# Extra identity products on TensorE between and inside the attention stages of a two-layer vision kernel

## The chip, the cores and the metric

The kernel runs on 1 core of one Trainium2 chip. The metric is device time in microseconds (us) for one execution over a batch of 8 images, the median of several runs. The engines are TensorE (PE; its weight loads are PEld in the profile), VectorE (DVE), ScalarE (ACT), GpSimd (POOL) and SyncE (SP), which issues the DMAs.

## The reference, cut to what matters

Layer 0 is a linear attention with a 5x5 depthwise convolution. Layer 1 is a sparse-linear attention, and all that is changed lies in it:

```python
qkv = einsum('oc,bcl->bol', qkv_w, xf)          # 4 heads of 64, 4096 tokens, 64 blocks of 64
blk_scores = einsum('bhnd,bhmd->bhnm', qb, kb)  # block means
_, lut = top_k(blk_scores, 6)
s = einsum('bhnqd,bhnkd->bhnqk', qr, kg) * scale
o_s = einsum('bhnqk,bhnkd->bhnqd', softmax(s), vg)     # over the 6 chosen blocks
kvb = einsum('bhmkd,bhmke->bhmde', softmax(k), vr)
kv_q = einsum('bhnm,bhmde->bhnde', 1 - sel, kvb)       # over the 58 others
o_l = num / (den + EPS)                                # softmax(q) times kv_q
o = einsum('oc,bcl->bol', out_w, o_s + proj(o_l))
```

All is f32.

## The kernel before

The program is written per engine; each engine runs its own list, and semaphores with counts order them. The outer loop runs over pairs of images; inside it both images are unrolled, and in each image layer 0, then layer 1 with four heads one after the other: 32 heads in a run. One head of layer 1 has these stages on PE, in `tensor`:

1. Tokens: 16 steps over 256 tokens each: q, k, v by eight f32 instructions (L778) into banks 0 and 1 of PSUM, and two steps later `turn` (L755, L762), which transposes q, k and their softmax features and forms the products of keys and values of each block for the linear part.
2. Waits: for `s_raw` (ACT has copied the last tokens out of banks 0 and 1), `s_tbe`, `s_kvd`, and for the first head of an image `s_sel`, followed there by two transposes of the selection (L797), whose result the second scores wait for.
3. `scores(0)` and `scores(1)` (L818): each four products of 64x64 by 192 columns, each product from gathered keys and values. The gathers go into four buffers: POOL copies six pieces (L561), ACT two, DVE four (both through their copy helpers, L982 and L1144). For steps from 4 on they wait for `s_o` of the step four before.
4. `complements()` (L847): 65 products of 64x64 by 64 columns, weights read from KVM with a stride of 65, in alternating halves of the output partitions, after eight DMAs have brought `kv_rows` back to SBUF (`s_rel`). ACT and DVE copy the result out by banks 4 to 7.
5. 32 softmax steps, in software pipeline: `scores(p)`, `turn_probs(p-1)` (L838, from step 8 on with a `turn_out`, L825) and `apply(p-2)` (L878 twelve and L884 four instructions). DVE takes the maxima (L1379), ACT the exponentials (L1088), ACT copies the turned probabilities (L982), `apply` raises `s_o`, for which DVE's, ACT's and POOL's gathers wait. Every third step DVE normalises (L1391, L1393, L1395).

DVE's order in a step is: load offsets, maxima(p), gather(p+2), and every third step normalise. ACT's is: copy probabilities (p-1), load offsets, exp(p), copy an output, gather(p+2).

Of the kernel before, what the change touches and what calls it, by code (L numbers as in the profile page):

```python
# [32 lines left out]
CH = 512  # L33
# [6 lines left out]
NP = NBLK // 2  # L40
# [57 lines left out]
def build(nc, x, w0, taps, wp, w1, wo, lw, lb, consts, out, n_batch):  # L98
    with ExitStack() as ctx:
# [3 lines left out]
        def sem(name):  # L103
            return ctx.enter_context(nc.semaphore(name))
# [7 lines left out]
        ident, same8, same_head = CST[:, 0:P], CST[:, P:2 * P], CST[:, 2 * P:3 * P]  # L112
# [10 lines left out]
        PS = ctx.enter_context(nc.psum_tensor("PS", [P, 8, CH], F32))  # L123
# [80 lines left out]
        def chunk_of(tile, c):  # L204

            f = 2 * c
            oy, ox = f // 8, (f % 4) // 2
            return tile.rearrange("p (f r c) -> p f r c", f=PL, r=PW)[:, f:f + 2, oy:oy + R, ox:ox + R]
# [81 lines left out]
        s_pt = sem("probs_stored")  # L290
# [31 lines left out]
        def settle(eng):  # L322

            eng.sem_inc(s_settled, 1)
# [248 lines left out]
        def _(pe):  # L574
            pe.wait_ge(s_w, 16 * 7)

            for h in range(NH):
                last = nc.tensor.matmul(PS[:, h // 2, (h % 2) * C:(h % 2 + 1) * C], lhsT=arena[0:D, 0:P],
                                        rhs=WO[0:D, h, :], start=True, stop=True)
            last.then_inc(s_wo, 1)  # L580
            for ot in range(KT):
                for h in range(NH):
                    last = nc.tensor.matmul(PS[:, 2 + ot, 0:1], lhsT=WO[0:D, h, ot * P:(ot + 1) * P],
                                            rhs=LB[0:D, :], start=(h == 0), stop=(h == NH - 1))
# [11 lines left out]
            with pe.Fori(0, n_batch // 2) as pair:  # L596
                for half in range(2):
# [12 lines left out]
                    for g in range(2):  # L610
# [67 lines left out]
                        for j in range(3):  # L678
                            for c in range(NCH):
# [5 lines left out]
                                for kt in range(KT):  # L685
                                    last = nc.tensor.matmul(bank(i),  # L686
                                                            lhsT=W0[:, kt, (2 * j + g) * P:(2 * j + g + 1) * P],
                                                            rhs=XN[:, kt, c * CH:(c + 1) * CH],
                                                            start=(kt == 0), stop=(kt == KT - 1))
# [10 lines left out]
                        for c in range(NCH + 2):  # L700
                            if c < NCH:
                                attend(1, c)
                            if c >= 2:
                                i = base + att_item(1, c - 2) + 1
                                pe.wait_ge(s_free[1], b * IT + 2 + count(i, 1))
                                for ot in range(KT):
# [3 lines left out]
                                                     rhs=chunk_of(RAW[0], c - 2), start=True, stop=False)  # L710
                                    hand(i, nc.tensor.matmul(bank(i), lhsT=WP[:, 2 + g, ot * P:(ot + 1) * P],
                                                             rhs=AGG[0][:, (c - 2) * CH:(c - 1) * CH],
                                                             start=False, stop=True))
# [21 lines left out]
                    for hp in range(2):  # L735
                        wait_emptied(pe, b, L0_ITEMS + D_ITEMS * hp - 1)
                        settle(pe)
                        for h in (2 * hp, 2 * hp + 1):
                            hd, hl = b * NH + h, h % 2

                            def turn(p):

                                pe.wait_ge(s_nrm, hd * TP + p + 1)
                                if p == 0:
                                    pe.wait_ge(s_scc, b + 1)
                                if p >= 2:
                                    pe.wait_ge(s_tbe, hd * TP + p - 1)
                                if p % 2 == 0 and p >= 4:
                                    pe.wait_ge(s_kvd, hd * 8 + p // 2 - 1)
                                if p == 2 and hl == 1:  # L750
                                    pe.wait_ge(s_one, hd * NP)
                                sg = SG[p % 3]
                                for u in range(2):
                                    for s in range(2):
                                        nc.tensor.transpose(PS[:, 2 + p % 2, (2 * s + u) * P:(2 * s + u + 1) * P],  # L755
                                                            sg[:, (4 * u + 2 * s) * D:(4 * u + 2 * s + 2) * D], ident)
                                at = 6 - 2 * (p // 2 % 2)
                                for u in range(2):
                                    j = 2 * (p % 2) + u
                                    for odd in range(2):  # L760
                                        rows = slice(D * odd, D * (odd + 1))
                                        last = nc.tensor.matmul(PS[D:P, at + odd, j * D1:(j + 1) * D1],  # L762
                                                                lhsT=sg[rows, (4 * u + 3) * D:(4 * u + 4) * D],
                                                                rhs=twos[rows, 2 * p + u, 0, D:KVW],
                                                                start=True, stop=True)
                                last.then_inc(s_tb, 1)

                            for p in range(TP):
# [6 lines left out]
                                for u in range(2):  # L775
                                    t = 2 * p + u
                                    for kt in range(KT):
                                        last = nc.tensor.matmul(  # L778
                                            PS[:, p % 2, u * 3 * D:(u + 1) * 3 * D], lhsT=XN[:, kt, t * P:(t + 1) * P],
                                            rhs=W1[:, kt, h, :], start=(kt == 0), stop=(kt == KT - 1))  # L780
# [5 lines left out]
                            turn(TP - 2)  # L786
                            turn(TP - 1)

                            pe.wait_ge(s_raw, (hd + 1) * TP)
                            pe.wait_ge(s_tbe, (hd + 1) * TP)  # L790
                            pe.wait_ge(s_kvd, (hd + 1) * 8)
                            if h == 0:
# [49 lines left out]
                            def complement(r, at, bank):  # L842
                                for k in range(8):
                                    for side in range(2):
                                        e = 16 * r + 8 * side + k
                                        if e < D1:
                                            last = nc.tensor.matmul(  # L847
                                                PS[D * side:D * (side + 1), bank, (at + k) * NBLK:(at + k + 1) * NBLK],
                                                lhsT=KVM[:, :, e], rhs=COMP[:, h * NBLK:(h + 1) * NBLK],
                                                start=True, stop=True)  # L850
                                last.then_inc(s_cq, 1)

                            def complements():
                                for k in range(8):
                                    pe.wait_ge(s_rel[k], (hd + 1) * 16)
                                pe.wait_ge(s_cmp, b + 1)
                                settle(pe)
                                for r in range(4):
                                    complement(r, 0, 4 + r)
                                pe.wait_ge(s_kqa, hd * 4 + 3)  # L860
                                pe.wait_ge(s_kqd, hd * 5 + 3)
                                settle(pe)
                                complement(4, 0, 6)
                                pe.wait_ge(s_kqa, hd * 4 + 2)
                                pe.wait_ge(s_kqd, hd * 5 + 2)

                            def apply(p):
                                pe.wait_ge(s_pt, hd * NP + p + 1)
                                t = p // 3
                                if p == 0:  # L870
                                    pe.wait_ge(s_kqa, (hd + 1) * 4)
                                    pe.wait_ge(s_kqd, (hd + 1) * 5)
                                if p % 3 == 0 and t >= 2:
                                    pe.wait_ge(s_on, hd * TRIOS + t - 1)
                                at = p % 3 * 2 * D1
                                for i in range(3):
                                    for blk in range(2):
                                        nc.tensor.matmul(  # L878
                                            PS[D * blk:D * (blk + 1), 6 + t % 2, at:at + D1],
                                            lhsT=PT[p % 2][:, i * P + D * blk:i * P + D * (blk + 1)],  # L880
                                            rhs=G[p % GD][:, blk, i, D:KVW], start=(i == 0), stop=(i == 2))
                                for blk in range(2):
                                    n = 2 * p + blk
                                    last = nc.tensor.matmul(  # L884
                                        PS[D * blk:D * (blk + 1), 6 + t % 2, at + D1:at + 2 * D1],
                                        lhsT=QO[hl][D:P, n * D:(n + 1) * D], rhs=KVQ[:, n, :],
                                        start=True, stop=True)
                                last.then_inc(s_o, 1)

                            for p in range(NP + 2):  # L890
                                if p < NP:
                                    scores(p)
                                if p == 1:
                                    complements()
                                if 1 <= p <= NP:
                                    turn_probs(p - 1)
                                if p >= 2:
                                    apply(p - 2)
# [9 lines left out]
                        for ot in range(KT):  # L908
                            for c in range(NCH):
                                i = L0_ITEMS + D_ITEMS * hp + NCH * ot + c  # L910
                                claim(i)
                                for hh in range(2):
                                    last = nc.tensor.matmul(bank(i), lhsT=WO[:, 2 * hp + hh, ot * P:(ot + 1) * P],  # L913
                                                            rhs=QO[hh][:, c * CH:(c + 1) * CH],
                                                            start=(hh == 0), stop=(hh == 1))
# [590 lines left out]
```

## Time and profile before

| | us |
|---|---|
| median of 3 runs | 9082.88 |
| lowest, highest | 9064.64, 9105.43 |
| profiled execution, its own time | 9057.69 |
| profiled execution, span | 9055.9 |
| mean granted clock of PE | 0.919 |
| PE busy | 7636.7 |
| DVE, POOL, ACT busy | 5037.9, 3786.7, 3520.5 |

The span reaches from the first to the last instruction of one profiled execution. A granted clock of 1.00 is 2.4 GHz, 0.50 is 1.2 GHz. Busy times of PE are of pipelined instructions whose ends are modelled, so a busy PE need not be one at its peak.

### The profile page before, as it was taken

To read this page: it belongs to the slowest core of one execution; us is meant where nothing else is said; L and a number is where in the kernel's file an instruction comes from. 1 tells how busy PE (TensorE), PEld (TensorE's weight loads), DVE (VectorE), ACT (ScalarE), POOL (GpSimd) and SP (SyncE) were. 2 spreads that over 40 slices of the span, in tenths; PEclk is the share of its full clock that TensorE was granted. 3 is DMA by queue.
4 is the path that set the end of the run, shared out by engine and by line. 5 is a ranking of instruction groups with operands and counts; after the bars stand their busy time and mean duration, and the time that the engine had idled before them with its cause. 6 is when DMAs were issued, how large, how long until landed. Compare 5 with 4: busy or idle time off the path is not lost.

```text
span 9055.9 us, 206227 instructions
## 1 busy us (share of the span) xinstructions
PE 7636.7 (84%) x65004; PEld 5190.5 (57%) x65004; DVE 5037.9 (56%) x11563; ACT 3520.5 (39%) x9207; POOL 3786.7 (42%) x10084
## 2 busy tenths in 40 slices
PE   8978799787997879978899778997789977799788
PEld 5655556555565555655555555565555555566555
DVE  3475644756447564475644756447564475644655
ACT  1145621445214552145521455215552155511555
POOL 2345533445334553345533444334443344533444
PEclk9988999888999889988999888998889988999888
DMA  3201122011220112201122111221112211122111
GB/s 101 65 16 26 41 87 65 16 26 38 89 65 16 27 42 85 65 18 26 51 75 65 21 22 49 77 65 21 23 53 73 65 22 22 57 68 65 24 20 55
DMA packets 398743, 431.90 MB, mean 48 GB/s; under 512 B 159184, under 2 KB 355984, under 8 KB 393296
## 3 DMA queue, kind: packets, MB, share of 16 engines
q1 hardware_dynamic: 397648, 418.42, 16.3%
q8 instruction: 550, 9.01, 0.4%
q14 instruction: 545, 4.46, 0.2%
HBM read 102.76 MB, written 67.63 MB: 19 GB/s over the span
## 4 chain that ended last, share of the span: by engine, by line
PE 54%; DVE 23%; issue 7%; DMA 6%; ACT 5%; DVEq 3%; SPq 1%; POOL 0%; ACTq 0%; POOLq 0%
PE PS L623 12%; PE PS L686 7%; DVE arena L1144 5%; PE PS L913 5%; DVE arena L1234 4%; PE PS L778 3%; PE PS L666 3%; PE PS L878 3%; PE PS L838 3%; PE PS L847 3%; DVE SM L1379 3%; ACT arena L1088 3%; DVEq L1367 2%; DMA kv_rows<-arena 2%; PE PS L654 2%
## 5 line engine op out<-in xcount | busy, mean ns | idle before, releaser
L982 ACT ACTIVATE arena<-PS 128x128 f32<-128x128 f32 (+5 forms) x4160 | 1552.0, 399 | 1947.5 <-PE PS L623 596.5
L561 POOL COPY arena<-arena 64x129 f32 x6144 | 1527.9, 291 | 1372.0 <-PE PS L884 1094.0
L485 POOL TENSOR_TENSOR arena<-arena 128x512 f32<-128x512 f32 x768 | 806.2, 1072 | 1459.5 <-PE PS L623 1443.6
L623 PE MATMUL PS<-arena 128*128 128x256 f32 x6144 | 1359.1, 379 | 46.4 <-DMA arena<-arena 46.3
L1144 DVE COPY arena<-PS 64x260 f32<-64x260 f32 (+2 forms) x1272 | 634.3, 515 | 1352.5 <-PE PS L623 524.7
L623 PEld LDWEIGHTS PS<-arena 128*128 128x128 f32 x6144 | 1155.4, 189 | 270.6 <-issue 98.0
L1144 DVE COPY arena<-arena 64x129 f32 x4096 | 840.9, 267 | 398.3 <-PE PS L884 285.9
L1234 DVE RECIPROCAL arena<-arena 128x512 f32<-128x512 f32 x256 | 857.5, 3350 | 119.1 <-ACT arena L1030 117.5
L818 PE MATMUL PS<-arena 64*64 64x192 f32 x8192 | 699.0, 386 | 256.9 <-POOL arena L561 242.0
L491 POOL TENSOR_TENSOR BUF<-BUF,arena 128x512 f32<-128x512 f32 x256 | 358.2, 1399 | 1282.3 <-ACT arena L1018 1282.3
L1379 DVE TENSOR_REDUCE SM<-PS 128x1 f32<-128x384 f32 x1024 | 570.6, 558 | 539.7 <-issue 434.3
L1088 ACT ACTIVATE arena<-PS,SM 128x384 f32<-128x384 f32 x1024 | 595.1, 581 | 638.9 <-DVE SM L1379 598.6
L778 PE MATMUL PS<-W,BUF 128*128 128x192 f32 x4096 | 818.7, 348 | 27.2 <-ACT BUF L1010 20.5
L778 PEld LDWEIGHTS PS<-W,BUF 128*128 128x128 f32 x4096 | 687.2, 197 | 63.2 <-ACT BUF L1010 21.2
L686 PE MATMUL PS<-BUF,W 128*128 128x512 f32 x1536 | 678.8, 604 | 37.5 <-DVE BUF L1207 33.7
L825 PE MATMUL PS<-CST,arena 128*128 128x128 f32 x1024 | 312.1, 337 | 415.9 <-ACT arena L1088 379.7
L838 PE MATMUL PS<-CST,arena 128*128 128x128 f32 x3072 | 589.2, 307 | 52.0 <-ACT arena L1088 51.2
L878 PE MATMUL PS<-arena 128*64 128x65 f32 x12288 | 632.8, 243 | 0.0
L538 POOL TENSOR_TENSOR arena<-arena,SM 128x256 f32<-128x256 f32 x512 | 314.4, 614 | 748.1 <-DVE SM L1322 746.7
L878 PEld LDWEIGHTS PS<-arena 128*64 128x64 f32 x12288 | 483.9, 149 | 196.1 <-issue 193.9
L1147 DVE TENSOR_SCALAR arena<-PS 128x256 f32<-128x256 f32 (+1 forms) x336 | 160.1, 477 | 733.0 <-PE PS L623 432.7
L666 PE MATMUL PS<-arena 128*128 128x512 f32 x1024 | 498.4, 608 | 68.8 <-DVE arena L1241 56.0
(102 smaller groups left out, 10563.4 us busy)
## 6 DMA issues: line engine op xcount, KB each, us to landing
arena<-arena SPq DMA_DIRECT2D x1024, 128.0 KB, 2.3
arena<-arena SPq DMA_DIRECT2D x768, 144.5 KB
BUF<-in_x SPq DMA_DIRECT2D x18, 2048.0 KB, 12.0
kv_rows<-arena SPq DMA_DIRECT2D x256, 130.0 KB, 3.5
arena<-kv_rows SPq DMA_DIRECT2D x256, 130.0 KB
out<-BUF SPq DMA_DIRECT2D x64, 512.0 KB, 2.6
arena<-in_taps SPq DMA_DIRECT2D x96, 288.0 KB, 3.6
W<-in_w SPq DMA_DIRECT2D x2, 768.0 KB, 5.8
```

The lines of the kernel that those rows point to most:

```text
L485: last = pool.tensor_tensor(o, tap, mix, ALU.mult)
L561: last = pool.tensor_copy(G[p % GD][0:D, j // 3, j % 3, :], KVB[0:D, bass.ds(off, KVW)])
L623: last = nc.tensor.matmul(bank(i)[:, a * 256:(a + 1) * 256], lhsT=TW[n % 2][:, a * CH + k * P:a * CH + (k + 1) * P], rhs=src[:, k // 2:k / ...
L686: last = nc.tensor.matmul(bank(i), lhsT=W0[:, kt, (2 * j + g) * P:(2 * j + g + 1) * P], rhs=XN[:, kt, c * CH:(c + 1) * CH], start=(kt == 0 ...
L778: last = nc.tensor.matmul(PS[:, p % 2, u * 3 * D:(u + 1) * 3 * D], lhsT=XN[:, kt, t * P:(t + 1) * P], rhs=W1[:, kt, h, :], start=(kt == 0) ...
L838: last = nc.tensor.transpose(PS[:, 4 + p % 2, i * P:(i + 1) * P], PR[p % 2][:, i * P:(i + 1) * P], ident)
L878: nc.tensor.matmul(PS[D * blk:D * (blk + 1), 6 + t % 2, at:at + D1], lhsT=PT[p % 2][:, i * P + D * blk:i * P + D * (blk + 1)], rhs=G[p % G ...
L982: return nc.scalar.activation(o, i, ACT.Copy)
L1088: nc.scalar.activation(PR[p % 2].rearrange("p (i s c) -> p s i c", i=3, s=2), PS[:, 2 * (p % 2):2 * (p % 2) + 2, 0:3 * D].rearrange("p s ( ...
L1144: return nc.vector.tensor_copy(o, i)
L1234: order.after(nc.vector.reciprocal(DN[c % 2], DN[c % 2]))
L1379: nc.vector.tensor_reduce(NM[:, p % 2:p % 2 + 1], PS[:, 2 * (p % 2):2 * (p % 2) + 2, 0:3 * D], AX.XY, ALU.max, negate=True).then_inc(s_nm, 1)
```

## The change

A helper `keep_clock(bank, n)` issues n f32 products of the 128x128 identity with its own first 112 columns into columns 400 to 511 of a bank of PSUM; nothing reads those columns. It is called with 20 products into bank 0 after the wait for `s_raw` that follows the last `turn` of each head, with 8 products into bank 7 at the head of `complements()`, and with 2 products into bank 6 or 7 in each `apply`, in front of the wait for `s_pt`, which moves behind the other waits of `apply`.

```diff
+                            def keep_clock(bank, n):
+                                for _ in range(n):
+                                    nc.tensor.matmul(PS[:, bank, 400:CH], lhsT=ident, rhs=ident[:, 0:CH - 400],
+                                                     start=True, stop=True)
+
                             pe.wait_ge(s_raw, (hd + 1) * TP)
+                            keep_clock(0, 20)
                             pe.wait_ge(s_tbe, (hd + 1) * TP)
...
                             def complements():
+                                keep_clock(7, 8)
                                 for k in range(8):
                                     pe.wait_ge(s_rel[k], (hd + 1) * 16)
...
                             def apply(p):
-                                pe.wait_ge(s_pt, hd * NP + p + 1)
                                 t = p // 3
                                 if p == 0:
                                     pe.wait_ge(s_kqa, (hd + 1) * 4)
                                     pe.wait_ge(s_kqd, (hd + 1) * 5)
                                 if p % 3 == 0 and t >= 2:
                                     pe.wait_ge(s_on, hd * TRIOS + t - 1)
+                                keep_clock(6 + t % 2, 2)
+                                pe.wait_ge(s_pt, hd * NP + p + 1)
```

## Rows read from the trace of the kernel before

**Rows 1.** The page: busy times, and the chain that ended last by engine

```profile
PE 7636.7 (84%) x65004; PEld 5190.5 (57%) x65004; DVE 5037.9 (56%) x11563; ACT 3520.5 (39%) x9207; POOL 3786.7 (42%) x10084
...
PE 54%; DVE 23%; issue 7%; DMA 6%; ACT 5%; DVEq 3%; SPq 1%; POOL 0%; ACTq 0%; POOLq 0%
```

**Rows 2.** Timeline of PE, third head of the first image: start, duration, idle before

```profile
884.82 1.12 PE L755 MATMUL PS<-CST,arena 128*128 128x128 f32 x4 [0.53 <-POOL arena L538]
...
891.66 0.92 PE L818 MATMUL PS<-arena 64*64 64x192 f32 x8 [5.10 <-POOL arena L561]
893.68 0.92 PE L818 MATMUL PS<-arena 64*64 64x192 f32 x8 [1.10 <-POOL arena L561]
896.32 8.00 PE L847 MATMUL PS<-arena 64*64 64x64 f32 x130 [1.72 <-DMA arena<-kv_rows]
...
907.25 0.92 PE L878 MATMUL PS<-arena 128*64 128x65 f32 x12
```

**Rows 3.** Windows (stretch, length; PE, PEld, DVE, ACT, POOL; PEclk, DMA, GB/s)

```profile
532.70:536.10 3.40, 3.40 (x12) 3.21 (x12) 2.40 (x18) 0.94 (x4) 0.92 (x3) 0.50 0.00 0
536.10:539.50 3.40, 3.40 (x33) 2.94 (x32) 2.79 (x10) 2.23 (x8) 1.55 (x5) 1.00 0.02 3
...
886.60:896.30 9.70, 1.84 (x16) 0.68 (x17) 4.11 (x16) 2.84 (x9) 5.49 (x23) 0.50 0.37 64
...
896.30:904.30 8.00, 7.98 (x131) 7.88 (x131) 2.24 (x4) 2.04 (x4) 1.48 (x6) 0.50 0.02 4
...
2033.40:2043.80 10.40, 9.98 (x94) 6.04 (x93) 5.35 (x20) 6.78 (x17) 3.26 (x14) 0.50 0.07 15
...
7353.40:7363.00 9.60, 8.42 (x94) 5.08 (x93) 5.24 (x21) 6.40 (x16) 2.94 (x12) 0.69 0.07 16
...
sum 318.50, PE 290.12 PEld 175.25 DVE 171.13 ACT 205.77 POOL 101.85; mean PE 9.07 PEld 5.48 DVE 5.35 ACT 6.43 POOL 3.18
...
4290.50:4357.30 66.80, 51.98 (x781) 34.66 (x781) 44.36 (x158) 46.67 (x132) 38.74 (x156) 1.00 0.06 12
...
8804.80:8881.00 76.20, 63.51 (x781) 42.30 (x781) 47.39 (x159) 46.70 (x132) 38.08 (x155) 0.78 0.05 11
...
sum 2220.90, PE 1749.97 PEld 1166.24 DVE 1447.10 ACT 1491.80 POOL 1236.05; mean PE 54.69 PEld 36.45 DVE 45.22 ACT 46.62 POOL 38.63
```

**Rows 4.** Products by themselves: two timeline rows, a source row, a window

```profile
524.61 3.67 PE L723 MATMUL PS<-arena,W 128*128 128x64 f32 x16 [4.27 <-DVE arena L1274]
...
880.69 0.60 PE L755 MATMUL PS<-CST,arena 128*128 128x128 f32 x4
...
L755 PE MATMUL PS<-CST,arena x2048: 272/273/477, 531.0 to 8924.7; 128*128 128x128 f32 x187
...
210.00:220.00 10.00, 10.00 (x219) 7.38 (x220) 3.79 (x10) 3.87 (x12) 0.00 (x0) 0.91 0.01 2
```

**Rows 5.** Timeline of PE and DVE, softmax steps of the third head, fourth image

```profile
4312.91 0.57 PE L878 MATMUL PS<-arena 128*64 128x65 f32 x12
...
4313.57 0.56 PE L818 MATMUL PS<-arena 64*64 64x192 f32 x8
...
4317.80 0.33 PE L825 MATMUL PS<-CST,arena 128*128 128x128 f32 x1 [0.99 <-ACT arena L1088]
...
4318.38 0.57 PE L878 MATMUL PS<-arena 128*64 128x65 f32 x12
...
4318.90 0.39 PE L818 MATMUL PS<-arena 64*64 64x192 f32 x2
...
4319.38 0.96 DVE L1144 COPY arena<-arena 64x129 f32 x4 [0.56 <-PE PS L884]
...
4320.43 0.57 PE L878 MATMUL PS<-arena 128*64 128x65 f32 x12
...
4320.91 0.56 DVE L1379 TENSOR_REDUCE SM<-PS 128x1 f32<-128x384 f32 x1 [0.57 <-issue]
...
4321.50 0.73 DVE L1144 COPY arena<-arena 64x129 f32 x4
```

## The prediction

> **What bounds the kernel now.** I began with the page: TensorE (PE) is busy 84% of the span and holds 54% of the chain that ended last, with VectorE (DVE) at 23%; the mean granted clock of PE is 0.92 of full speed [rows 1]. So I asked where the clock is at 0.5 and whether PE is what is waited for there. The timeline of PE through one head's change from tokens to attention shows it: after the last turned pair PE idles 5.1 us until GpSimd's (POOL's) gather frees the first scores, runs 0.9 us, idles 1.1, runs 0.9, idles 1.7 us for the last DMA of `kv_rows`, and then issues the 130 complement instructions in 8.0 us, then the first steps [rows 2]. The windows, made for each of the 32 heads, give the clock of each part: between tokens and complements 19 of 32 heads are wholly at 0.50 and the rest at 0.56 to 0.71; the complements are at 0.50 in all 32; the first four softmax steps are at 0.50 to 0.70; the other 28 are between 0.78 and 1.00 [rows 3]; one or two of each 32 stand there. Idleness lets the clock fall, and the complements, though PE shows busy for all of their 8 us, do not lift it. It rises only in the dense steps after them.
>
> In those 28 steps (66.8 us where the clock stays up [rows 3]) PE is not simply the bound. The timeline of three of them has DVE waiting on the products (`apply`), PE waiting on ScalarE's (ACT's) exponentials, and ACT on DVE's maxima [rows 5]: a ring over all three, 7.2 us for three steps (3 x 66.8 / 28).
>
> **The price of a product.** An f32 product is two matmul instructions (four score products show as x8), each with its weight load, and identity weights are 128 wide. Nearest rows [rows 4]: at low clock 16 instructions with 128x128 weights and 64 columns take 3.67 us, at most 0.23 us each, and 0.22 without the tail of the last; at full clock four transposes with 128 weights and 128 columns take 0.60, so (0.60 - 0.273) / 3 = 0.109 each. 112 columns lie between 64 and 128, so the load sets the pace in both. One product is 0.22 us at full clock and 0.43 at half: 20 products 4.4 or 8.7 us, 8 products 1.7 or 3.5, two products 0.44 or 0.87. Nothing is removed; 20 + 8 + 64 products times 32 heads add 2944 products, 5888 instructions.
>
> **The 20 products.** They follow the last `turn` directly (its copy was long done) and lie in the 5.1 us idle of PE. At full clock they fit: no cost. At half clock all 20 would end 3.6 us late. But they are a dense run of full-array products, of the kind under which the stretch 532.70 to 536.10, with PE 3.40 of 3.40 busy at 0.50, ended its low clock: the next stretch is at 1.00 [rows 3]; the forecast is that the clock comes back in their middle, so the first scores are about 1.5 us late, which the second scores, waiting for their own gather until 2.0 us later, take up. In the first head of a batch the transposes of SEL also move behind them; the second scores, which need their result, wait for POOL anyway. Cost nothing.
>
> **The 8 products.** From the end of the second scores to the complements is 1.7 us in the head shown. At full clock they fill it exactly; at half they make the complements 1.8 us late. The DMAs are on SP's queue and depend on nothing that moved. I take 0.4 us per head (some heads low, some with a shorter gap): +13 us. Bounds 0 and 58.
>
> **Complements at full clock.** No row shows it. Bounds: half of 8.0, 3.9 us, if the array sets their pace at both clocks; 130 x 45.7 ns = 5.9 us by the window at 210 us, where PE issues 219 mostly small matmuls in 10 us [rows 4]; 8.0 us if something unclocked (their weights are read with a stride of 65) sets it. The `apply` group of twelve took 0.92 us low and 0.57 at full clock [rows 2, 5], a ratio of 0.62, which would be 5.0. I take 4.9: 3.1 us less. It will not hold in every head: the clock can still fall between the first and second scores, or under the complements themselves, which have a quarter of the array each. For 0.88 of it: 2.7 us x 32 = -87 us. Bounds 0 and -125.
> The Trainium skill, "TensorE: Matmul & The Clock Gate", section "Wait — 56ns, not 53.3ns?", says that with hardware decode off the sequencer's microcode spends about 62 ns on each MATMUL and that this binds once the array work is shorter. By that rule the complements would take 130 x 62 ns = 8.1 us at either clock and the saving would be nothing; the 8.00 us measured at half clock agrees with it, the 45.7 ns of the window at 210 us does not.
>
> **The first four steps** took 318.5 us over 32 heads, 9.95 each; 10.4 where wholly low, 9.6 where low for 0.31 x 2 x 9.6 = 6.0 us [rows 3]. So a low us costs 0.8 / 4.4 = 0.18 us, and at full clock they would take 8.5; two of their three product pairs lie on the path, +0.9. I take a gain of 1.0: -32 us. Bounds 0 and -46.
>
> **The other 28 steps, clock.** Nine of the 32 stretches have a mean clock of 1.00 and take 66.5 to 67.9 us, mean 67.0; the longest, at 0.78, takes 76.2 [rows 3]. With PE busier the falls should go: 2220.9 - 32 x 67.0 = -77 us.
>
> **The other 28 steps, the two products.** Their cover would be PE's idle time, but they sit between `turn_probs` and `apply`, and `apply` waits for nothing there (18.38 after the turn at 17.80). In the ring I hold the turn at 4317.80 and walk on [rows 5]: `apply` 18.38 becomes 18.82 and ends 0.44 later, DVE's gather, idle 0.56 for it, goes from 19.38 to 19.82; the next maxima from 20.91 to 21.35, ending 21.91; the next `apply`, 20.43, becomes 20.87 to 21.0 and ends 21.70 to 21.9; the gather after it goes from 21.50 to 21.94. The third gather of the three comes late by DVE's own work (the normalisation), and has no wait that grows. So three steps cost at least 0.44; if the next scores start later after `apply` (0.66 as at 4312.91 to 4313.57, not 0.52 as at 4318.38 to 4318.90) PE makes the following turn late too, and it is 0.57. I take 0.50: 28 / 3 = 9.3 groups, 4.65 us a head, +149 us. Bounds: 0 if all is absorbed in PE's idle time (PE is busy 52.0 of 66.8 us), and 28 x 0.44 x 32 = +394 if every one is on the path; from the walk, 131 to 170.
>
> **Sum.** +13 - 87 - 32 - 77 + 149 = -34 us against the profiled execution, span 9055.9 of 9057.7 us. The median of the runs, 9082.9, is 25 us above it; the same difference gives 9049.
>
> **Rivals.** (1) The complements do not speed up. For: 8.00 us in every head and a strided weight load; against: the 45.7 ns window. The sum loses 87 us: 9136. (2) The clock falls again in the 3.6 us between the 20 products and the 8, in which PE runs only two score groups, and the half-speed 8 delay the complements. For: the low clock of the head shown is there in its last `turn` already (four transposes in 1.12 us), right after an idle time of 0.5 us [rows 2, 4]. Then no gain on complements, half of that on the first steps, and +1.8 x 32 = 58 instead of 13: 9049 + 87 + 16 + 45 = 9197. It ends slower, and decides once more than about half of the heads do it. (3) The pairs in the steps are absorbed, because PE, ACT and DVE regroup around them: a third of 149 is left, 9049 - 99 = 8950. For: PE's 14.8 us of idle per head in these steps; against: the walk. (4) Two or three crossings of the ring in three steps: 0.8 us per group, 0.3 x 9.3 x 32 = +89: 9138.
>
> **How the numbers follow.** Chances: forecast 0.50, its own range 9000 to 9095; rival 1 0.15; rival 2 0.12; rival 3 0.15; rival 4 0.08. The term that decides is a difference of 149 + 13 lost and 196 gained, so the middle is near no change. The range from rival 3 to just short of rival 2, 8955 to 9150, leaves out about 2 in 10. A measurement here tells 0.5%, 45 us. Faster (below 9037): rival 3 and 0.5 of the forecast's, 0.40. Slower (above 9128): rivals 1, 2 and 4 with a part of each inside, and the forecast's tail, 0.25. Within: 0.35.
>
> **What would show it.** In the changed profile: complements at clock 1.0 in most heads with a duration of 4 to 6 us; the first scores no later than before relative to the last turn; the 28 steps at clock 1.00 in nearly all heads, but 71 to 72 us long instead of 66.8; four or so new instructions ahead of each `apply`, 0.44 us between turn and `apply` added. Complements at 8.0 us with clock 1.0 say rival 1; at clock 0.5, rival 2; 28 steps at 68 us, rival 3; above 74, rival 4.

## The result and the profile after

The changed kernel takes 9222.3 us (median of 4 runs, 9202.0 to 9227.2) against 9076.4 us for the kernel before in the same comparison: ratio 1.0152, 95% interval 1.0122 to 1.0181. It is slower by 1.5%, where 9049 us and "near no change" were forecast, and it lies outside the range of 8955 to 9150. In the changed kernel the new products are L791, the scores L824, the turns L831 and L844, the complements L853 and `apply` L886 and L892; in the experiments the numbers move by a few lines.

The page of the changed kernel, busy times and chain:

```profile
PE 8114.3 (88%) x70892; PEld 5833.8 (63%) x70892; DVE 5070.5 (55%) x11563; ACT 3519.4 (38%) x9207; POOL 3801.9 (41%) x10084
...
PE 55%; DVE 23%; issue 8%; ACT 5%; DVEq 3%; DMA 3%; SPq 1%; POOL 1%; POOLq 0%; ACTq 0%
```

PE's mean granted clock rose from 0.919 to 0.952, PE is busy 478 us more, and the span is 160.8 us longer (9216.7). The higher clock did not shorten the run. The new products (L791) are 908.5 us of PE's busy time.

The timeline of PE in the third head again, start and duration, as in [rows 2]:

```profile
892.95 6.88 PE L791 MATMUL PS<-CST 128*128 128x112 f32 x40
899.75 1.03 PE L824 MATMUL PS<-arena 64*64 64x192 f32 x16
900.71 2.04 PE L791 MATMUL PS<-CST 128*128 128x112 f32 x16
902.95 7.94 PE L853 MATMUL PS<-arena 64*64 64x64 f32 x130 [0.19 <-issue]
910.82 0.55 PE L844 MATMUL PS<-CST,arena 128*128 128x128 f32 x3
911.29 0.56 PE L824 MATMUL PS<-arena 64*64 64x192 f32 x8
```

This is the picture that was hoped for: the 20 products (x40 instructions) begin at low clock and end at full, both score groups run in 1.03 us, the 8 products take 2.04, and the first turn takes 0.55. Only the complements are as long as ever: 7.94 us, where they took 8.00. The windows (columns as in [rows 3]) of this head's complements and first four steps, of another head's complements, and of the 28 steps of the head of [rows 5] are below; the sums are over the 32 heads, in this order: last turn to complements, first four steps, 28 steps:

```profile
902.90:910.90 8.00, 7.96 (x131) 7.92 (x132) 2.26 (x4) 2.06 (x4) 1.48 (x6) 1.00 0.02 5
...
910.80:919.70 8.90, 7.45 (x105) 5.38 (x104) 5.14 (x21) 6.79 (x17) 2.97 (x12) 1.00 0.08 18
...
2877.30:2885.40 8.10, 8.10 (x132) 7.98 (x132) 2.30 (x4) 2.09 (x4) 0.00 (x0) 0.71 0.01 2
...
4370.20:4442.40 72.20, 61.66 (x897) 47.39 (x897) 45.85 (x160) 46.70 (x132) 39.01 (x156) 1.00 0.05 12
...
sum 361.80, PE 309.92 PEld 278.89 DVE 144.46 ACT 90.83 POOL 214.23; mean PE 9.69 PEld 8.72 DVE 4.51 ACT 2.84 POOL 6.69
...
sum 339.60, PE 310.41 PEld 222.11 DVE 169.76 ACT 204.79 POOL 100.88; mean PE 9.70 PEld 6.94 DVE 5.31 ACT 6.40 POOL 3.15
...
sum 2328.00, PE 1970.07 PEld 1515.13 DVE 1473.43 ACT 1492.80 POOL 1247.01; mean PE 61.56 PEld 47.35 DVE 46.04 ACT 46.65 POOL 38.97
```

The same three sums before were 319.5 (the answer of the windows before, not shown ahead), 318.5 and 2220.9 [rows 3]. So the 161 us are: way to the complements +42, complements 0 (256.1 us over the 32 heads before, 256.6 after), first four steps +21, 28 steps +107, all the rest -10. Six of the 32 complement windows have clock 1.00, two 0.50, the others lie between; all take 7.9 to 8.1 us. Five heads have clock 1.00 through their first four steps as well, and take 8.5 to 8.9 us for them.

In the 28 steps the clock is at full speed nearly throughout, and the head of [rows 5] takes 72.2 us for 66.8. Two of its steps on the timeline, PE and DVE:

```profile
4399.36 0.33 PE L831 MATMUL PS<-CST,arena 128*128 128x128 f32 x1 [1.00 <-ACT arena L1096]
...
4399.85 0.60 PE L791 MATMUL PS<-CST 128*128 128x112 f32 x4
...
4400.38 0.57 PE L886 MATMUL PS<-arena 128*64 128x65 f32 x12
...
4401.38 0.94 DVE L1152 COPY arena<-arena 64x129 f32 x4 [1.00 <-PE PS L892]
...
4401.97 0.60 PE L791 MATMUL PS<-CST 128*128 128x112 f32 x4
...
4402.49 0.57 PE L886 MATMUL PS<-arena 128*64 128x65 f32 x12
...
4402.91 0.56 DVE L1387 TENSOR_REDUCE SM<-PS 128x1 f32<-128x384 f32 x1 [0.60 <-issue]
...
4403.50 0.74 DVE L1152 COPY arena<-arena 64x129 f32 x4
```

From the turn (4399.36) to `apply` (4400.38) it is now 1.02 us, where it was 0.58 (4317.80 to 4318.38 in [rows 5]): the pair's 0.44, as priced. DVE's idle time for `apply` grew from 0.56 to 1.00 us, the same 0.44. Nothing hides the pair: it lies on the ring of PE, DVE and ACT.

### The profile page after: what moved, and what is told of

It reads as the page before. It is cut to its first block, busy times and chain, and to the rows that moved or that the text cites. A ratio compares the mean times of both kernels' runs of the same rounds, so it can differ in the third digit from the quotient of the medians.

```text
span 9216.7 us, 217683 instructions
## 1 busy us (share of the span) xinstructions
PE 8114.3 (88%) x70892; PEld 5833.8 (63%) x70892; DVE 5070.5 (55%) x11563; ACT 3519.4 (38%) x9207; POOL 3801.9 (41%) x10084
## 4 chain that ended last, share of the span: by engine, by line
PE 55%; DVE 23%; issue 8%; ACT 5%; DVEq 3%; DMA 3%; SPq 1%; POOL 1%; POOLq 0%; ACTq 0%
PE PS L623 12%; PE PS L686 7%; DVE arena L1152 5%; PE PS L921 5%; PE PS L791 4%; DVE arena L1242 4%; PE PS L778 3%; DVE SM L1387 3%; PE PS L666 3%; PE PS L853 3%; PE PS L886 3%; ACT arena L1096 2%; PE PS L844 2%; DVEq L1375 2%; PE PS L654 2%
## 5 line engine op out<-in xcount | busy, mean ns | idle before, releaser
L1152 DVE COPY arena<-arena 64x129 f32 x4096 | 871.9, 274 | 447.3 <-PE PS L892 335.2
L791 PE MATMUL PS<-CST 128*128 128x112 f32 x5888 | 908.5, 293 | 0.0
L791 PEld LDWEIGHTS PS<-CST 128*128 128x128 f32 x5888 | 820.8, 209 | 16.9 <-issue 11.5
L824 PE MATMUL PS<-arena 64*64 64x192 f32 x8192 | 654.1, 352 | 49.3 <-POOL arena L561 25.0
L831 PE MATMUL PS<-CST,arena 128*128 128x128 f32 x1024 | 293.8, 318 | 351.9 <-ACT arena L1096 316.3
L844 PE MATMUL PS<-CST,arena 128*128 128x128 f32 x3072 | 541.7, 287 | 62.9 <-ACT arena L1096 62.1
L886 PE MATMUL PS<-arena 128*64 128x65 f32 x12288 | 595.7, 233 | 0.0
L990 ACT ACTIVATE arena<-arena 64x129 f32 x2048 | 519.3, 300 | 115.8 <-POOL arena L524 47.0
```

What stands on the lines that cost most here:

```text
L791: nc.tensor.matmul(PS[:, bank, 400:CH], lhsT=ident, rhs=ident[:, 0:CH - 400], start=True, stop=True)
L886: nc.tensor.matmul(PS[D * blk:D * (blk + 1), 6 + t % 2, at:at + D1], lhsT=PT[p % 2][:, i * P + D * blk:i * P + D * (blk + 1)], rhs=G[p % G ...
L990: return nc.scalar.activation(o, i, ACT.Copy)
L1152: return nc.vector.tensor_copy(o, i)
```

## The experiments

In all of them the ratio is to the kernel before, timed beside them.

**steps_only and front_only** split the change: the first takes out the 20 and the 8, the second the pair.

```diff
-                            keep_clock(0, 20)
-                                keep_clock(7, 8)
...
-                                keep_clock(6 + t % 2, 2)
```

> The change with the 20 and the 8 products taken out; only the pair ahead of each apply stays. Theory A (the pair lies on the ring of TensorE, VectorE and ScalarE): the 28 steps take 72 to 73 us per head at clock 1.00 as in the changed kernel, against 69.4 before, so +107 us, and the first four steps, still begun at low clock, cost up to 1 us more per head: ratio to the kernel before 1.012 to 1.016. Theory B (the loss lies in the 20 and 8 products, which make scores and complements late): the ratio is 1.00 to 1.005.

> The change with the pair in each apply taken out; the 20 and the 8 products stay. Theory A: the way from the last turn to the complements is 41 us longer over 32 heads as in the changed kernel, the complements stay at 8.0 us, the steps keep their low stretches: ratio 1.002 to 1.006. Theory B: the whole loss is here, ratio 1.012 to 1.016.

steps_only: 1.0116 (1.0092 to 1.0141). front_only: 1.0031 (1.0014 to 1.0049). Theory A holds: about four fifths of the loss is the pair in the steps. The 28 steps of steps_only, over 32 heads, and below them the same of front_only:

```profile
sum 2329.80, PE 1970.30 PEld 1515.85 DVE 1472.60 ACT 1491.44 POOL 1238.38; mean PE 61.57 PEld 47.37 DVE 46.02 ACT 46.61 POOL 38.70
```

```profile
sum 2227.40, PE 1758.88 PEld 1172.16 DVE 1443.89 ACT 1488.47 POOL 1237.43; mean PE 54.97 PEld 36.63 DVE 45.12 ACT 46.51 POOL 38.67
```

With the pair 72.8 us a head, without it 69.6. The first four steps, in the same order:

```profile
sum 349.90, PE 322.58 PEld 229.94 DVE 172.53 ACT 204.37 POOL 101.63; mean PE 10.08 PEld 7.19 DVE 5.39 ACT 6.39 POOL 3.18
```

```profile
sum 309.30, PE 276.58 PEld 167.29 DVE 169.50 ACT 207.22 POOL 100.03; mean PE 8.64 PEld 5.23 DVE 5.30 ACT 6.48 POOL 3.13
```

Against 318.5 before, the pair alone costs +31 us there, 0.98 us a head, and the 20 and the 8 alone, through the clock, bring only -9. Together that is the +21 of the changed kernel.

**step_one**: `keep_clock(6 + t % 2, 1)` in place of 2 in steps_only.

> steps_only with one product in place of two ahead of each apply. If the price is what lies between turn and apply on the ring, half of it: 28 steps of about 70 us (72.8 with two, 67.0 with none at full clock), ratio 1.003 to 1.007. If any product at this place costs (a wait, not a length), nearly 72.8 again and a ratio above 1.010.

1.0015 (1.0003 to 1.0027), less than expected; the 28 steps:

```profile
sum 2237.20, PE 1810.46 PEld 1333.31 DVE 1464.30 ACT 1490.92 POOL 1239.68; mean PE 56.58 PEld 41.67 DVE 45.76 ACT 46.59 POOL 38.74
```

That is 69.9 us a head. At full clock: 67.0 with none (the mean of the nine stretches of the prediction), 69.9 with one, 72.8 with two. The price is linear in the length, 2.9 us a head for 0.22 us, as if it were on the path in 13 of 28 steps (2.9 / 0.22), or 1.4 times in three.

**steps_moved** puts the pair where PE waits, without the 20 and the 8:

```diff
                             def turn_probs(p):
                                 x = p - TURN_LAG
-                                pe.wait_ge(s_p, hd * NP + p + 1)
                                 if p >= 2:
                                     pe.wait_ge(s_pt, hd * NP + p - 1)
                                 if x >= 2:
                                     pe.wait_ge(s_one, hd * NP + x - 1)
+                                keep_clock(4 + p % 2, 2)
+                                pe.wait_ge(s_p, hd * NP + p + 1)
...
-                                keep_clock(6 + t % 2, 2)
```

> No 20 and no 8 products; the pair of each step is moved from in front of apply to in front of turn_probs' wait for the exponentials (waits for the PSUM bank first), into the bank that the turn is about to overwrite. If what costs is the place between turn and apply, TensorE's idle time ahead of the turn (0.42 us per step in the kernel before) covers most of the pair, while the clock stays up: 28 steps of 67 to 69 us per head, ratio 0.990 to 0.999. If any pair in a step costs (TensorE is the bound by its load alone), 72 us again and a ratio of 1.012 or more.

0.9941 (0.9916 to 0.9965): the same number of products per step, 32 heads, and the sign turns. The 28 steps fall to 67.9 us a head, with no low clock left in them:

```profile
sum 2171.80, PE 2063.88 PEld 1523.30 DVE 1439.65 ACT 1478.28 POOL 1231.39; mean PE 64.50 PEld 47.60 DVE 44.99 ACT 46.20 POOL 38.48
```

PE is busier here than in steps_only (2064 against 1970 us) and the steps are 158 us shorter. So neither the load of PE nor the clock sets the loss, but the place of the pair between turn and `apply`.

**after_apply** issues the pair behind `apply`, also without the 20 and the 8:

```diff
-                                keep_clock(6 + t % 2, 2)
...
                                 last.then_inc(s_o, 1)
+                                keep_clock(2 * ((p + 1) % 2), 2)
```

> No 20 and no 8 products; the pair of each step is issued behind apply instead of ahead of it, into a free bank of the scores. Same instructions and the same load of TensorE as steps_only. If the ring turn, apply, gather is the price, it is gone here: 28 steps of 67 to 69 us, ratio 0.990 to 0.998. If the load of TensorE is, or the scores that now start 0.44 us later, 71 to 73 us and 1.008 to 1.013.

My expectation fell: 1.0326 (1.0308 to 1.0343), the slowest of all. The 28 steps take 75.0 us a head and the first four 13.8; the sums over 32 heads, 28 steps and then first four:

```profile
sum 2401.60, PE 2323.09 PEld 1663.08 DVE 1515.42 ACT 1476.20 POOL 1194.64; mean PE 72.60 PEld 51.97 DVE 47.36 ACT 46.13 POOL 37.33
```

```profile
sum 440.30, PE 426.95 PEld 278.60 DVE 184.25 ACT 218.55 POOL 133.59; mean PE 13.34 PEld 8.71 DVE 5.76 ACT 6.83 POOL 4.17
```

The timeline of PE, one step at full clock:

```profile
4454.28 0.57 PE L883 MATMUL PS<-arena 128*64 128x65 f32 x12
...
4454.77 0.33 PE L889 MATMUL PS<-arena 64*64 64x65 f32 x4
...
4455.04 0.70 PE L791 MATMUL PS<-CST 128*128 128x112 f32 x4
...
4455.67 0.56 PE L823 MATMUL PS<-arena 64*64 64x192 f32 x8
...
4456.15 0.33 PE L830 MATMUL PS<-CST,arena 128*128 128x128 f32 x1
```

From `apply` to the next scores it is 1.39 us (4454.28 to 4455.67), against 0.52 to 0.66 without the pair [rows 5]: a pair between two groups of 64x64 costs 0.73 to 0.87 us of PE, up to twice its 0.44 ahead of `apply`. The products start 0.27 us after the last 64x64 group started, where score groups overlap with it, and the scores wait 0.63 us from their start. In the stretch shown PE's own work repeats every 2.46 us (scores 4453.20 to 4455.67), 28 x 2.46 = 68.9 us, with no wait for another engine in it: here PE is nearly the bound. So this run does not test the ring; it tests the price of a product among small tiles, which I had taken from rows of full-array neighbours.

That price is not why this run is the slowest. The eleven heads whose 28 steps ran at clock 1.00 took 71.4 to 72.3 us, mean 71.7, a little less than the 72.8 of steps_only. The other 21 had mean clocks of 0.81 to 0.99 and took up to 83.6 us, and the first four steps, at 0.50 throughout in 21 heads, took 440.3 us against 349.9 of steps_only. In the first head a step at half clock took 4.07 us of PE (scores 595.36 to 599.43), where it took 2.46 at full. Why the clock stayed low for longer here is not shown.

**Fewer products, later.** moved_one is steps_moved with one product; moved_late has the pair and moved_one_late one product, both only from the fourth turn on (`if p >= 4:` ahead of `keep_clock`).

> As steps_moved (no 20, no 8, products in front of turn_probs' wait), with one product per step. If the clock is the only thing that helps, and one product is enough to hold it up, the 28 steps take at most the 67.9 us of steps_moved, at best 67.0, and the first steps lose less at low clock: ratio 0.990 to 0.994. If one is not enough, stretches with a clock below 1.0 come back and the ratio is between 0.994 and 1.0.

> As steps_moved, with the pair only from the fourth turn on. The turn behind the complements was 1.0 us later per head with the pair in front of it at low clock (8.92 from the first complement to the first turn, 7.93 before): that comes back, 32 us: ratio 0.990 to 0.992 (0.994 with it). If the early pairs pay for themselves by lifting the clock sooner, the ratio stays at 0.994 or above.

> One product per step, only from the fourth turn on. If both savings add: ratio 0.988 to 0.991, the fastest of all; 28 steps at 67.0 to 67.9 us.

moved_one: 0.9913 (0.9897 to 0.9930). moved_late: 0.9946 (0.9928 to 0.9964). moved_one_late: 0.9908 (0.9891 to 0.9925), 8968.7 us, the lowest median of the kernels that compute the reference, though not told apart from moved_one (8971.6). One product is enough: 28 steps at 67.1 us a head in both, sum for moved_one_late:

```profile
sum 2147.40, PE 1961.62 PEld 1362.71 DVE 1414.46 ACT 1491.00 POOL 1246.88; mean PE 61.30 PEld 42.58 DVE 44.20 ACT 46.59 POOL 38.97
```

Leaving out the early ones is worth nothing that can be told: the turn behind the complements comes 1 us sooner, but the first four steps are longer (331.9 against 320.7 us for the pair, 320.5 against 312.6 for one), because their clock comes back later. The expectation of 0.990 to 0.992 for moved_late was missed.

**sel_first** is front_only with `keep_clock(0, 20)` moved behind the waits for `s_tbe` and `s_kvd` and behind the transposes of the selection.

> front_only with the 20 products behind the transposes of the selection and behind the waits for s_tbe and s_kvd. If the longer way to the complements in the first head of each image (13.9 us against 10.1 before) comes from those transposes being queued behind the 20 products, that way shrinks to 10 to 11.5 us in these eight heads, and the ratio falls from 1.003 to 0.999 to 1.001. If it comes from the scores waiting for TensorE itself, it stays at 13 us or more and the ratio at 1.003.

1.0010 (0.9997 to 1.0022), with front_only at 1.0031. In the first head of the first image, changed kernel first, then sel_first:

```profile
569.51 4.72 PE L791 MATMUL PS<-CST 128*128 128x112 f32 x40
...
574.16 0.33 PE L803 MATMUL PS<-CST,arena 64*128 64x64 f32 x2
574.53 0.93 DVE L1368 TENSOR_SCALAR arena<-PS 64x64 f32<-64x64 f32 x4 [4.12 <-PE PS L803]
576.23 0.93 DVE L1152 COPY arena<-arena 64x129 f32 x4 [0.77 <-issue]
577.51 0.92 PE L824 MATMUL PS<-arena 64*64 64x192 f32 x8 [3.02 <-POOL arena L561]
...
579.82 3.75 PE L791 MATMUL PS<-CST 128*128 128x112 f32 x16
```

```profile
572.10 0.30 PE L802 MATMUL PS<-CST,arena 64*128 64x64 f32 x2 [1.12 <-DVE arena L1151]
572.33 4.72 PE L791 MATMUL PS<-CST 128*128 128x112 f32 x40
576.98 0.56 PE L824 MATMUL PS<-arena 64*64 64x192 f32 x8
578.66 0.56 PE L824 MATMUL PS<-arena 64*64 64x192 f32 x8 [1.12 <-POOL arena L561]
579.14 2.04 PE L791 MATMUL PS<-CST 128*128 128x112 f32 x16
581.11 3.16 PE L853 MATMUL PS<-arena 64*64 64x64 f32 x50
```

In the changed kernel the transposes (L803) stand behind the 20 products, DVE sits 4.12 us for them, and its four gathers for the first scores come behind the complement masks (L1368) on its queue. PE then idles 3.02 us ahead of the first scores, and the 8 products run at half speed, 3.75 us. With the order turned round the complements start 10.4 us after the last turn in these eight heads, on average, instead of 14.2 (10.2 before). In the other 24 heads, which have no such transposes, the way is 10.6 us against 10.2 in front_only, so part of the gain is lost there; the later start of the 20 products, behind the two other waits, was not tested by itself. (The trace puts the 3.02 us down to a gather of POOL; of the three gathers for the first scores DVE's ended last, at 577.16.)

**contig_weights** asks why the complements do not speed up. The edit reads their weights side by side instead of every 65th: the same elements of the same buffer, grouped otherwise. The sums over blocks are then of other numbers; everything else is the changed kernel.

```diff
-                                                lhsT=KVM[:, :, e], rhs=COMP[:, h * NBLK:(h + 1) * NBLK],
+                                                lhsT=FOLD[0:D, e * D:(e + 1) * D], rhs=COMP[:, h * NBLK:(h + 1) * NBLK],
```

> The changed kernel, but the complements read their weights from 64 neighbouring columns instead of every 65th (the sums over blocks are then of other numbers, so this part of the output is not the reference's); same number and shapes of instructions. If the strided read keeps the complements at 8.0 us at full clock, they now take 4 to 5 us where the clock is 1.0, and the ratio falls from 1.015 to about 1.003. If each instruction has its own cost whatever it reads, they stay at 7.9 to 8.0 us and so does the ratio.

> A repeat look at the changed kernel with the complements' weights read from neighbouring columns (that part of the output is of other numbers): 4.2 to 4.4 us at full clock, 7.3 at half, as in the first look at it.

0.9980 (0.9968 to 0.9992), against 1.0152: in the changed kernel the strided read carries 1.7%, more than expected, as the first four steps shrink too. The timeline and window of one head's complements:

```profile
897.00 4.21 PE L853 MATMUL PS<-arena 64*64 64x64 f32 x130 [0.27 <-issue]
```

```profile
897.00:901.20 4.20, 4.20 (x130) 4.00 (x130) 2.30 (x4) 2.10 (x4) 1.35 (x6) 1.00 0.02 4
```

and the durations (min, median, max in ns) of the complement's weight loads, first in the changed kernel, then with contiguous weights:

```profile
L853 PEld LDWEIGHTS PS<-arena x4160: 187/210/236, 583.5 to 9094.7; 64*64 64x64 f32 x199
```

```profile
L853 PEld LDWEIGHTS PS<-arena x4160: 129/135/228, 585.1 to 8936.7; 64*64 64x64 f32 x199
```

The strided load takes 210 ns at either clock, the contiguous one 135 at full. (Loads overlap, so these are not the times from one to the next.) The 130 instructions come every 61 ns with stride and every 32 ns without, at full clock. The repeat of this run (the second expectation; in spite of its label it is the changed kernel with that edit) gave the same 135 ns and one execution of 9059.4 us. The first four steps shrink from 339.6 to 287.1 us over 32 heads, and 27 heads have clock 1.00 there: the complements are over before the clock falls under them.

Stride and clock work together. Two heads of contig_weights ran their complements at 0.50, and there the contiguous ones took 7.3 and 7.2 us (load 223 ns, an instruction every 56 ns), only 0.7 less than the strided ones. In the kernel before, with all its complements at 0.50, contiguous weights by themselves would by that have brought about 0.7 us a head, an estimate; no run tests it.

**contig_front_moved** joins the parts: sel_first's 20 and 8 products, one product per step as in moved_one_late, contiguous weights (that part of the output is again of other numbers).

> What the change could have been: 20 products behind the transposes of the selection, 8 ahead of the complements, one product per step in front of turn_probs from the fourth on, and the complements' weights read from neighbouring columns (that part of the output is of other numbers). If the gains add (ratio 0.991 for the steps, 1.001 for the front, 3.5 us per head from the complements and 1 to 1.5 us per head from the first steps at full clock), the ratio is 0.972 to 0.982. If the front still costs more than it brings, 0.985 or above.

0.9739 (0.9723 to 0.9755), 8829.9 us: the gains add. The complements take 4.2 to 4.5 us a head, the first four steps 271.1 us over 32 heads, the 28 steps 2145.8. Only the way to the complements is longer than before, 336.5 us for 319.5.

## Why the prediction was wrong

- **Price of a product: right** where its neighbours use the full array (40 instructions in 4.72 us; 0.44 us added between turn and `apply`), and that the clock comes back in the middle of the 20. Too low by up to a factor of two among 64x64 tiles, a place that the change does not use.
- **Complements at full clock: the step that failed most.** "I take 4.9: 3.1 us less" rested on `apply`'s ratio and on the window at 210 us, both without such a stride. They took 8.0 us at full clock: -87 us became 0. This was rival 1, and its "for" named the stride; contig_weights shows it as the cause. I gave it 0.15. The Trainium skill ("TensorE: Matmul & The Clock Gate", section "Wait — 56ns, not 53.3ns?") has about 62 ns per MATMUL with hardware decode off, which gave the prediction's estimate of 8.1 us. The number came out, but that rule is not the reason: with contiguous weights the same 130 instructions come every 32 ns. (The prediction's lower bound, "half of 8.0, 3.9 us", should read 4.0; nothing hangs on it.)
- **First four steps: wrong in sign,** -32 forecast, +21 measured. The working does not give its own result: 9.95 - (8.5 + 0.9) is 0.55 us a head, -18 us, and not 1.0. The price of the pairs, 0.9 a head, came out at 0.98 (steps_only), in part by luck: they ran mostly at low clock, and at clock 1.00 the heads with pairs take 8.5 to 8.9 us, those of front_only without them 8.0 to 8.3. What failed is the clock's share, which brought 9 us (front_only) where 46 were counted at full clock: in 26 of 32 heads the clock is low under some or all of the complements, and the steps mostly start low. With contiguous weights, 287 us, -31.
- **28 steps, clock: right.** Low stretches are gone; moved_one shows the whole 74 us of it (2220.9 to 2146.7).
- **28 steps, the pair: right in mechanism, too small.** Forecast +149 (0.50 per three steps), measured 2328.0 - 32 x 67.0 = +184, which is 0.62 per three. The walk held one crossing of the ring in three steps plus a part; step_one and steps_only give 1.4. This term alone is 35 us. It went the way of rival 4, though not as far as its 0.8.
- **The 20 and 8: too cheap,** +42 for +13. "The second scores, which need their result, wait for POOL anyway" was the fault: it looked at PE and not at DVE's queue, where the masks stand ahead of the gathers. The first heads of the eight images (not of a batch, as the prediction has it) lost 32 of the 42 us there, and sel_first gives 31 of them back. The other 24 heads lost 0.44 us each, as the forecast's 0.4.
- Together: 87 + 53 + 35 + 29 us of misses, less 10 elsewhere, make up the 195 us between -34 and +161, to rounding. Rival 1 alone, at 9136, would still have been inside the range; it took the other terms, all missed in the same direction, to leave it.

Rival 2's fall of the clock came, but mostly under the complements. Ahead of them it is seen in the first head of an image shown above, whose 8 products ran at half speed. Rival 3 was wrong here and is right when the product stands in front of a wait.

Left open: what in the strided weight read sets 61 ns (no other stride was tried), what lets the clock fall under the complements, and how contiguous weights could be had with the right numbers without a costlier copy or DMA; that wasn't tried.

## What to carry to other kernels

In this kernel filler work was nearly free only directly in front of a wait that is long enough, and not between two dependent pieces of a ring: the same pair per step cost 1.2% or gave 0.6%, by its place alone. Before paying for a higher clock, ask whether the stage that ran at low clock is bound by the clock, and look for what in its operands differs from the rows that the ratio is taken from. When an instruction is moved behind filler, follow its consumer's whole queue, not only its own result.

## What the hardware showed beyond that

- Weights read with a stride of 65 f32 made a 64-wide load take 210 ns at both clocks, and contiguous ones 135 ns at full and 223 ns at half clock. The 130 complement instructions took 8.0 us at both clocks with the stride, and 4.2 and 7.3 us without it.
- In the first head of the changed kernel the granted clock was 1.00 from 584 to 586 us, under the complements and right after the full-array products, and 0.50 from 587 us on, while PE was busy for all of the complements' 8.0 us (583.5 to 591.5, mean 0.71). Where they began at 0.50, as in all 32 heads before and two after, it stayed there to their end.
- A pair of full-array products between 64x64 groups took 0.73 to 0.87 us of PE, and 0.44 between full-width groups, at full clock.
